# Cross-attention on one core: query row sums moved to TensorE, check products moved to batch 14, and the later queries split and spread by themselves

## What is computed

```python
Q = relu(queries @ Wq + bq);  K = relu(keys @ Wk + bk);  V = relu(values @ Wv + bv)
scores = einsum('hbqd,hbkd->hbqk', Qh, Kh) * scale
key_mask = sign(abs(sum(keys, axis=-1)))
scores = where(key_mask == 0.0, NEG, scores)
attn = softmax(scores, axis=-1)
q_mask = sign(abs(sum(queries, axis=-1)))
attn = attn * q_mask[..., None]
out = einsum('hbqk,hbkd->hbqd', attn, Vh)   # heads side by side again
return out + queries                         # queries is x; keys and values are both ctx_1024
```

## Time and profile before

| | |
|---|---|
| median of 3 runs | 380.84 us (379.0 to 381.56) |
| profiled execution, its own time | 380.48 us |
| its span, first to last instruction | 378.7 us |
| TensorE matmul busy | 357.3 us, 94% of the span |
| ScalarE busy | 303.9 us, 80% |
| VectorE busy | 240.4 us, 63% |
| GpSimd busy | 5.7 us, 2% |
| mean granted TensorE clock | 0.995 |

### The profile page before, as it was taken

One profiled execution on the slowest core, in us unless ns is written; L12 is line 12 of the kernel. 1 busy time (PEld: TensorE's weight loads), 2 busy tenths in 40 slices (PEclk: granted clock), 3 DMA queues, 4 the chain that ended last, 5 costly groups with the idle time before them and its releaser, 6 DMA issues.

```text
span 378.7 us, 16915 instructions
## 1 busy us (share of the span) xinstructions
PE 357.3 (94%) x6712; PEld 252.0 (67%) x6712; DVE 240.4 (63%) x785; ACT 303.9 (80%) x405; POOL 5.7 (2%) x20
## 2 busy tenths in 40 slices
PE   7997898799999999999999999999999999799991
PEld 5655666467676767676776767676776767577660
DVE  5797948267593939576684939485775937475202
ACT  2487477678888888888888888888888888689990
POOL 4010000000000000000000000000000000000000
PEclk9999999999999999999999999999999999999997
DMA  7529904956383745646373846547363837245100
GB/s 222 137 76 326 340 7 88 335 190 209 109 286 86 271 130 185 212 153 191 134 243 85 303 99 221 178 159 227 126 210 103 295 89 263 62 151 175 13 3 8
DMA packets 42852, 63.42 MB, mean 167 GB/s; under 512 B 28426, under 2 KB 32842, under 8 KB 42826
## 3 DMA queue, kind: packets, MB, share of 16 engines
q1 hardware_dynamic: 42106, 62.15, 51.8%
q10 hardware_dynamic: 720, 0.89, 0.7%
HBM read 14.55 MB, written 0.82 MB: 41 GB/s over the span
## 4 chain that ended last, share of the span: by engine, by line
PE 82%; DVE 6%; SPq 3%; DMA 3%; issue 2%; ACT 1%; DVEq 0%; ACTq 0%
PE psum L564 31%; PE psum L549 26%; PE psum L516 12%; PE psum L508 11%; SPq L334 3%; DMA k_parts<-k_low 3%; PE psum L636 1%; DVE v_biased L810 1%; PE psum L647 1%; DVE values L820 1%; DVE selectors L989 1%; ACT probs L477 1%; ACT k_parts L467 1%; DVE q_sum L946 1%; SPq L301 1%
## 5 line engine op out<-in xcount | busy, mean ns | idle before, releaser
L477 ACT ACTIVATE probs<-psum 128x800 f32<-128x800 f32 x384 | 293.5, 840 | 53.3 <-PE psum L549 53.3
L564 PE MATMUL psum<-probs,values 128*32 128x200 f32 x3072 | 153.7, 333 | 0.0
L549 PEld LDWEIGHTS psum<-query_bd,k_parts 64*128 64x128 f32 x1536 | 96.1, 187 | 44.9 <-issue 40.0
L564 PEld LDWEIGHTS psum<-probs,values 128*32 128x32 f32 x3072 | 97.8, 110 | 40.8 <-issue 19.1
L549 PE MATMUL psum<-query_bd,k_parts 64*128 64x200 f32 x1536 | 120.0, 286 | 1.6 <-DMA k_parts<-k_low 1.4
L773 DVE TENSOR_SCALAR_CACHE_REDUCE k_raw<-psum,bk_sb 128x361 f32<-128x361 f32 (+2 forms) x63 | 37.7, 600 | 88.3 <-PE psum L508 88.2
L508 PE MATMUL psum<-keyT,wk_mixed 128*32 128x361 f32 (+2 forms) x504 | 52.4, 491 | 6.2 <-DMA keyT<-in_ctxT 2.2
L516 PE MATMUL psum<-wv_sb,keyT 128*32 128x129 f32 x1536 | 55.1, 277 | 3.3 <-DVE v_biased L810 3.3
L820 DVE TENSOR_SCALAR values<-v_biased,keep 128x128 f32<-128x128 f32 x192 | 43.8, 289 | 6.4
L516 PEld LDWEIGHTS psum<-wv_sb,keyT 128*32 128x32 f32 x1536 | 38.4, 109 | 10.8 <-DVE v_biased L810 4.0
L810 DVE TENSOR_TENSOR v_biased<-psum,bv_sb 128x384 f32<-128x384 f32 x64 | 35.1, 548 | 0.0
(11 more groups left out here) (64 smaller groups left out, 81.7 us busy)
## 6 DMA issues: line engine op xcount, KB each, us to landing
k_parts<-k_high SPq DMA_DIRECT2D x30, 722.0 KB, 5.0
k_parts<-k_low SPq DMA_DIRECT2D x30, 722.0 KB, 5.5
keyT<-in_ctxT SPq DMA_DIRECT2D x15, 722.0 KB, 4.4
query_rep<-k_parts SPq DMA_DIRECT2D x4, 800.0 KB, 8.0
residual<-in_x SPq DMA_DIRECT2D x64, 12.5 KB
out<-residual SPq DMA_DIRECT2D x64, 12.5 KB
x_sb<-in_x SPq DMA_DIRECT2D x1, 800.0 KB
values<-in_xT ACTq DMA_DIRECT2D x1, 600.0 KB, 6.7
```

The source lines that it names most:

```text
L477: nc.scalar.activation(probs[:, u % PROB_SLOTS], scores_ps[:, u % SCORE_SLOTS, :, 0:QCOLS], ACT.Exp, scale=SCALE).then_inc(probs_ready, 1)
L549: mm = nc.tensor.matmul(scores_ps[:, u % SCORE_SLOTS, j, n * TCOLS:(n + 1) * TCOLS], k_parts[rows, parity, t, kt * P:(kt + 1) * P], query_ ...
L564: mm = nc.tensor.matmul(o_spans[c * VCOLS:(c + 1) * VCOLS, half, :, :, 0:SPAN], values[:, parity, kt, half * HALF_PAIRS + c, :], probs[:, ...
```

## The change

The line numbers of the diff's minus side are those of the kernel before. What it does:

- **Row sums by TensorE.** x is no longer loaded to `x_sb`, and the two sums on VectorE go. In cycle 0 of batch 0, behind the first scores and ahead of the first key quarter, TensorE multiplies the 16 blocks of `xT_sb` (128 x 100) with a column of ones into `work_ps` (`sum_queries`). VectorE compares them with zero. In cycle 7 of batch 0 TensorE multiplies the mask with a 0/1 matrix `row_pick`, which GpSimd makes, in 4 matmuls (`pick_rows`), and VectorE copies the result to `row_mask`. The 16 small DMAs go.
- **Check products in batch 14.** `k_max` gets a column for each batch. `q_max`, all 16 products and the head sums are made once, behind the last values of batch 14.
- **Later queries apart.** `q_high` and `q_low` hold only batches 0 to 3, and the four DMAs at L351 copy those alone. Batches 4 to 15 get `late_high` and `late_low`, made by VectorE between the key quarters of batch 2 in batch 0, and four more DMAs, which SyncE issues behind `spread_keys(2, 0)`. `batch(b, ...)` on VectorE waits for them ahead of `spread_queries(b + 1, ...)`, in every batch from 1 on.
- **Order at the start.** Weights are mixed ahead of the selectors on VectorE. On ScalarE's DMA queue bk comes first, then the first block of xT, then Wq, bq and the rest of xT. On SyncE the loads of `residual` for batches 0 and 1 come right behind the first evacuations.
- **First batch on VectorE.** Reading and masking values is woven between the steps of the key split.

```diff
-            def spread_masks():
-                sp.wait_ge(q_masked, 1)
-                sp.wait_ge(pads_zeroed, 4)
-                ... 16 DMAs row_mask<-q_mask
@@ SyncE
             load_keys(1, 1)
-            sp.dma_start(x_sb[:], x.rearrange("b q d -> q b d")).then_inc(x_loaded, 16)
-            sp.wait_ge(q_relued, 2)
-            for ready, count, source, slots in ((q_high_ready, 1, q_high, (0, 1)), (q_split, 3, q_low, (2, 3))):
+            sp.wait_ge(pads_zeroed, 4)
+            sp.wait_ge(first_evacuated, KCHUNKS)
+            load_residual(0, 0)
+            load_residual(1, 1)
+            for ready, count, source, slots in ((q_relued, 2, q_high, (0, 1)), (q_split, 2, q_low, (2, 3))):
...
             spread_keys(1, 1)
-            spread_masks()
-            load_residual(0, 0)
-            load_residual(1, 1)
-            sp.wait_ge(work_filled, KPARTS + VGROUPS)
+            sp.wait_ge(work_filled, SUMS + KPARTS + VGROUPS)
             load_keys(3, 1)
             sp.wait_ge(scores_ready, UNITS)
             spread_keys(2, 0)
+            for ready, source, slots in ((late_high_ready, late_high, (0, 1)), (late_split, late_low, (2, 3))):
+                sp.wait_ge(ready, 1)
+                for n in slots:
+                    sp.dma_start(query_rep[n:P:SLOTS, :, QB * SQ:].bitcast(F32),
+                                 source[:].rearrange("p g n -> p (g n)").bitcast(F32)).then_inc(late_replicated, 16)
@@ GpSimd
+            nc.gpsimd.memset(row_pick, 1.0).then_inc(rows_picked, 1)
+            nc.gpsimd.affine_select(out=row_pick, in_=row_pick, ...).then_inc(rows_picked, 1)
@@ TensorE
+            def sum_queries(index):
+                work(index)
+                for b in range(B):
+                    mm = nc.tensor.matmul(work_ps[0:SQ, b:b + 1], xT_sb[:, b * SQ:(b + 1) * SQ], ones[:, 0:1],
+                                          start=True, stop=True)
+                mm.then_inc(work_filled, 1)
+            def pick_rows(index):
+                work(index)
+                pe.wait_ge(rows_picked, 2)
+                for g in range(SPANS):
+                    mm = nc.tensor.matmul(work_ps[:, g * B:(g + 1) * B], row_pick[:, g, :], q_mask[:],
+                                          start=True, stop=True)
+                mm.then_inc(work_filled, 1)
...
-            FIRST_SIDE_WORK = (((0, NEXT),), ((1, NEXT), (2, NEXT)), ((3, NEXT), VALUES[0]), VALUES[1:2], VALUES[2:3],
-                               (VALUES[3], KEYS[0]), KEYS[1:3], KEYS[3:4])
+            FIRST_SIDE_WORK = (((SUM, NEXT), (0, NEXT)), ((1, NEXT), (2, NEXT)), ((3, NEXT), VALUES[0]), VALUES[1:2],
+                               VALUES[2:3], (VALUES[3], KEYS[0]), KEYS[1:3], (KEYS[3], (ROWS, NEXT)))
@@ VectorE
-            def bound_scores(b, parity):
-                at = slice(b, b + 1) if isinstance(b, int) else bass.ds(b, 1)
-                v.tensor_tensor(bound_terms[:, at], k_max[:, parity:parity + 1], q_max[:, at], ALU.mult
-                                ).then_inc(bound_made, 1)
+            def bound_scores():
+                v.tensor_reduce(q_max[:], queryT[:].rearrange("p (b q) -> p b q", b=B), AX.X, ALU.max
+                                ).then_inc(q_maxed, 1)
+                dve.wait_ge(q_maxed, 1)
+                dve.wait_ge(k_max_ready, 2 * B)
+                v.tensor_tensor(bound_terms[:], k_max[:], q_max[:], ALU.mult).then_inc(bound_made, 1)
...
@@ VectorE, batch(b, ...) from batch 1 on
+                dve.wait_ge(late_replicated, 16 * SLOTS)
                 spread_queries(b + 1, 1 - parity)
                 finish_keep(b + 1, 1 - parity)
-                bound_scores(b + 1, 1 - parity)
```

More of the change, by code:

```diff
@@ L127, in attention @@
         k_chunk_max = sb("k_chunk_max", [P, KPARTS])
-        k_max = sb("k_max", [P, 2])
+        k_max = sb("k_max", [P, B])
+        late_high = sb("late_high", [P, QGROUPS - 1, QB * SQ], F32R)
+        late_low = sb("late_low", [P, QGROUPS - 1, QB * SQ], F32R)
         v_biased = sb("v_biased", [P, VGROUPS, VGROUP, D])
@@ L387, in general @@
             def general(b):
+                sp.dma_start(g_x, row(x, b)).then_inc(g_x_loaded, 16)
                 sp.dma_start(keyT[:, 0, 0:SK], row(ctxT, b)).then_inc(g_loaded, 16)
@@ L594, in side_work @@
                     k, ahead = step
-                    if keys or ahead == NEXT:
+                    if k == SUM:
+                        sum_queries(used)
+                        used = used + 1
+                    elif k == ROWS:
+                        pick_rows(used)
+                        used = used + 1
+                    elif keys or ahead == NEXT:
                         prepare(b + ahead, (parity + ahead) % 2, k, used)
@@ L600, in batch @@
                     units = range(cycle * CYCLE, (cycle + 1) * CYCLE)
-                    for step in side[cycle][:-1]:
+                    early = 0 if first and cycle == 0 else max(len(side[cycle]) - 1, 0)
+                    for step in side[cycle][:early]:
                         side_work(step)
@@ L607, in batch @@
                         pe.wait_ge(first_k_spread, KCHUNKS * QUADS)
-                    for step in side[cycle][-1:]:
+                    for step in side[cycle][early:]:
                         side_work(step)
@@ L868, in finish_outputs, with split_keys @@
                 v.tensor_tensor(residual[:, parity], residual[:, parity], o_norm[:], ALU.add).then_inc(out_ready, 1)
[L870 to L880 removed]
+            def split_keys(b, used):
+                max_keys(b, used)
+                turn_outputs(b - 2)
+                dve.wait_ge(k_replicated, 16 * SLOTS * (b - 1))
+                center_keys(k_high, b, k_high_ready)
+                center_keys(k_cent, b, k_cent_ready)
             def finish_keys(b, part):
@@ L909, in first_batch @@
                 spread_queries(1, 1)
+                finish_values(1, 1, 3, used + 3)
                 finish_keep(1, 1)
-                bound_scores(0, 0)
-                bound_scores(1, 1)
-                sum_heads()
                 used = used + VGROUPS
-                for c in range(KPARTS):
-                    read_keys(2, c, used + c)
-                split_keys(2, 0, used + KPARTS)
-                dve.wait_ge(rows_masked, 16 * HALF_PAIRS * SPANS)
+                read_keys(2, 0, used)
+                high_queries()
+                read_keys(2, 1, used + 1)
+                read_keys(2, 2, used + 2)
+                low_late_queries()
+                read_keys(2, 3, used + 3)
+                used = used + KPARTS
+                read_rows(used)
+                split_keys(2, used)
             def batch(b, parity, last=False, keys=True):
@@ L937, in batch @@
                         read_keys(b + 2, c, used + c)
-                    split_keys(b + 2, parity, used + KPARTS)
+                    split_keys(b + 2, used + KPARTS)
                 else:
+                    bound_scores()
+                    sum_heads()
                     turn_outputs(b)
-            def sum_queries(part):
-                rows = slice(part * B // 2, (part + 1) * B // 2)
-                dve.wait_ge(x_loaded, 16)
-                v.tensor_reduce(q_sum[:, rows], x_sb[:, rows], AX.X, ALU.add).then_inc(q_summed, 1)
@@ new lines, in low_first_queries, with low_late_queries @@
+            def low_first_queries(at):
+                v.tensor_tensor(q_low[:, at], queryT[:, at], q_high[:, at].bitcast(F32), ALU.subtract
+                                ).then_inc(q_split, 1)
+            def high_queries():
+                dve.wait_ge(q_relued, 1 + QGROUPS)
+                v.tensor_copy(late_high[:].rearrange("p g n -> p (g n)"), queryT[:, QB * SQ:]
+                              ).then_inc(late_high_ready, 1)
+            def low_late_queries():
+                dve.wait_ge(late_high_ready, 1)
+                v.tensor_tensor(late_low[:].rearrange("p g n -> p (g n)"), queryT[:, QB * SQ:],
+                                late_high[:].rearrange("p g n -> p (g n)").bitcast(F32), ALU.subtract
+                                ).then_inc(late_split, 1)
```

143 lines of the change are left out of this document (62 added, 81 removed).

## The result

The changed kernel takes 391.24 us in the median of 4 runs (389.49 to 393.58), beside 380.63 us for the kernel before (379.0 to 381.56): a ratio of 1.0305, 95% interval 1.0259 to 1.0351. It is slower, and it lies outside the range of the prediction. The profiled execution took 393.58 us with a span of 391.8, 13.1 more than the span before, at a mean granted clock of 0.963 (before 0.995). It is the slowest of the four runs, 2.3 us above their median.

The account below looks back on a forecast made before the run. TensorE was taken as the bound, at 21.07 us a loop batch, with only the start and batches 0 and 1 affected. A net +2.9 us at batch 2's start, added to 380.5, gave 383.4 us, range 379.6 to 387.5.

Parts of the forecast that it names:

- Start: Before batch 0: mixing goes ahead of the casts but Wq lands later, TensorE beginning at about 6.8 us; +0.4 us.
- Sums of queries: Batch 0, ahead of the first key quarter: 32 weight loads on TensorE, hidden by nothing; 2.7 us, from 1.8 to 3.5.
- my +0.3: Batch 0's net change after sums, picking, new waits and freed old waits; +0.3 us, from -0.7 to +1.2.
- Rows picked: Last cycle of batch 0: 4 TensorE matmuls, 8 passes of 128 loaded columns; 0.9 us.
- Batch 1, what goes: VectorE's mask wait, batch 3's late keys and SyncE's delay of batch 2's keys vanish; batch 1 alone would take 21.1 us.
- Batch 1, what comes: VectorE waits for late copies landing at 73.2, TensorE waits 7.0 us; net +2.9 us at the start of batch 2.
- rival 2: Batch 1: late copies crawl at 258 GB/s, landing at 76.3; 386.5 us, 388 with upper bounds elsewhere; chance 0.20.
- Batches 2 to 14 at nothing: Loop batches' small extra VectorE work fits about 0.6 us of slack, batch 14's checks fit 7.08 us idle; no cost.
- rival 3: Near the end, VectorE's batch 13 stall moves to where it has time; 381.3 us, 2.1 less; chance 0.10.
- my three signs of being wrong: SyncE issues late copies before the low keys are ready, they exceed 400 GB/s, or a loop batch changes.

Follow-up runs that it names:

- experiment 1: Changed kernel with SyncE issuing the four late query copies ahead of the key pair of batch 2; 379.14 us, 0.9967 of the kernel before.
- experiment 4: Changed kernel with each of the 16 sum matmuls moving 32 columns of ones in place of one; 390.5 us, 1.0269 of the kernel before.
- experiment 5: Changed kernel with 42 unread filler matmuls on TensorE ahead of batch 1's second key quarter, its batches 1 and 2 written out; 388.16 us, 1.0233 of before.
- experiment 6: Kernel before with only its 16 mask copies replaced by TensorE's row picking; 377.32 us, 0.9911 of the kernel before.
- Experiment 2: Changed kernel without VectorE's wait for the late copies in batches 1 and 2, those batches written out on VectorE; 378.4 us, 0.9954 of before.
- the wide sums: Sum matmuls moving 32 columns of ones in place of one: on the changed kernel 390.5 us, with late copies ahead of the key pair 378.98 us.
- experiment 7: Changed kernel with late copies ahead of the key pair, x loaded again and its row sums made by one VectorE reduction; 375.84 us, 0.9873 of before.
- experiment 3: Changed kernel with one matmul of 16 columns in place of the 16 sum matmuls, for timing alone; 386.13 us, 1.0154 of the kernel before.
- experiment 9: As experiment 7, but x asked for later, behind the last key chunk of batch 0; 374.41 us, 0.9874 of the kernel before.
- experiment 8: As experiment 7, but the start's loads and weight mixing in the order of the kernel before; 376.12 us, 0.9891 of the kernel before.
- the repetition of experiment 1: Changed kernel with late copies ahead of the key pair and one-column sums, run again beside the wide sums on the same chip; 379.06 us.
- experiment 10: As experiment 9, but VectorE's loop over batches 1 to 12 written out; 370.79 us, 0.9774 of the kernel before.

## Why the prediction was wrong

The mechanism named in it was right at every link of batch 1; its sizes were not, and one whole term was missing. In spans, my sum held +0.4 + 0.3 + 2.2 (batch 1) = +2.9, and the profile shows +13.1.

- *Start*: taken at +0.4, measured +0.6, and TensorE began at 6.71 (I had 6.8). Part of this is luck. Wq landed at 5.92, not at 6.55, and then its copy took 0.71 us beside GpSimd's pattern selection, where the copy before took 0.26. And two things move the first full product from profile to profile by more than the term: whether the first projection takes 0.94 or 1.70 us, and the half clock from 8 to 11. Like beside like, the new order costs what I took: 25.61 against 25.06 where the projection takes 1.70 (experiment 1, before), 24.17 and 24.24 against 23.73 where it takes 0.94 at full clock (experiments 4 and 5 against 6). Experiment 2, where the later xT kept TensorE waiting, is left out of this.
- *Sums of queries*: 2.7 us taken, 4.15 measured; with the clock at 1.00 they take 3.0 (0.094 a load, from the wide sums). The loads were sized nearly right; at a falling clock the same ones took 1.15 more and the matmuls behind them 1.8 more (31.97 - 28.99 = 2.98 in all; in three of the five profiles only 1.4 to 1.6). With the full clock batch 0 would be +0.7, against my +0.3. Rows picked: 0.9 taken, 1.07 measured.
- *Batch 1, what goes*: right. No wait for keyT, for k_parts or for the mask copies; experiment 6 shows it alone.
- *Batch 1, what comes*: the low keys were ready 6.7 us behind the transposing, as I had it (57.85 to 64.58). From there to the last landing I took 12.2 us and it took 14.3, that is 2.1 more. The likeliest place of these is visible, not tested: I gave the queue 5.6 us for the key pair and then only bytes, but SyncE alone needed from 64.61 to 71.16 to ask for the copies, and the last took 7.67 from there. As a rate, 3.94 MB in 14.3 us is 276 GB/s, nearer to rival 2's 258 than to the 322 of my 12.2 us.
- *The term that was missing*: TensorE's clock. Behind the wait it cost 2.4 (experiment 5), during and behind the sums 3.0 in this profile (experiment 4).
- *Batches 2 to 14 at nothing*: a loop batch stayed at 21.07 and batch 14 hid its new work. Rest grew by 2.1 in this profile: batch 13 took 25.20 us and not 23.26, as its stall was 0.3 longer and the clock fell behind it where it had not before. That is rival 3's place with the other sign, and chance has a part in it: experiments 1, 2 and 5 have the stall without the half clock.

Together, from prediction to profile: 0.2 + 3.4 + 2.1 + 2.4 + 2.1 = 10.2, and 383.4 + 10.2 = 393.6, the profiled execution. The failed step is that I gave the matmuls behind the wait and behind the sums the lengths of their rows of before, so that TensorE's clock stood in the sum at nothing. The half clock makes 3.0 + 2.4 + 1.6 = 7.0 of the 10.2 us in this profile, the late landing 2.1. In the median of the four runs the time is 7.8 above the forecast, and the scatter of these clock terms is the likeliest reason that it is less than 10.2 (argued, not shown). Rival 2, slower copies, was nearly right about the landing and had the right sign; its sizes without the clock ended at 388. None of my three signs of being wrong appeared (early copies, over 400 GB/s, another loop batch), so they would not have caught the error.

Beyond the sizes, I took the wait on `late_replicated` in batches 1 and 2 as given by the data. It isn't. Had I asked which queries are the first to lie in the late columns (those of batch 4, which VectorE spreads in batch 3), the fix would have stood in the prediction.

The price of the parts, as far as the runs separate them: the picked rows give some 3 us (experiment 6). The rest of VectorE's new order in batch 0, that is the later split of the queries, the woven values, the moved check products and one sum in place of two, gives a further 3.6 us (29.25 - 25.63, experiments 6 and 7); these four were not separated. The TensorE sums take back 5.1 us by the medians of experiment 3, 6.3 by batch 0 of the profile (31.97 - 25.63) and 3.3 by the medians of experiments 1 and 7. The early wait costs 12 (experiment 1).

## What to carry over

When work is taken out of a transfer queue and other work put in, write down for each wait which iteration first reads what it guards: here a wait two iterations early cost 12 us, although the copies themselves cost nothing. When a change leaves TensorE idle for several us, or gives it matmuls that no row of before resembles, read the granted clock behind them, and keep a second term for it (here 2.4 us behind 9.1 us of waiting, and 1.4 to 3.0 with the sums). Compare batch lengths, not totals, since the second cost can fall elsewhere, and compare medians of two chips only through the kernel before on each. When TensorE is the bound, a small reduction is cheaper on an engine that is idle at that place, as VectorE was in experiment 7.

## What the runs showed of the hardware

- Granted clock: with 9.12 us of idleness TensorE was granted 1.00 up to 75 us and 0.50 from 76 to 86; with fillers 1.00 throughout. With one moving column a weight load of 100 columns stepped 0.093 us at 1.00 (2.99 us for 32, experiment 1), and the clock fell to 0.50 in five of five profiles; with 32 columns the step was 0.094 and it fell in none of two.
- Shorter idle times have no certain price. TensorE idled 1.7 to 2.8 us at the stall near the end in the thirteen profiles that have one. Behind it the granted clock fell to 0.50 in seven (the changed kernel, experiments 6 to 9 and both with wide sums) and stayed at 1.00 in six. At the start it fell behind 1.83 and 1.87 us of idleness (the changed kernel and the repetition of experiment 1), where the first key projection then took 4.33 and 4.30 us; with 0.8 to 1.7 us of idleness it stayed at 1.00 in all others.
- At a granted clock of 1.00 the first projection (two passes of 400 columns) took 1.70 us in some profiles (before, experiment 1) and 0.94 in others (experiment 6, at 6.49 us). Experiments 1 and 4 have the same program up to the first full product, which came at 25.61 us (projection 1.70) and at 24.17 (projection 0.94). So 1.4 us between two profiles at the start need not be the effect of an edit.
- In every kernel with a VectorE loop, VectorE stood once behind it with nothing to wait for: 3.1 to 3.8 us in batch 13, and in experiment 2, whose loop begins two batches later and ends at the same one, 1.94 us at the start of TensorE's batch 14. With its loop written out it did not stand at all (experiment 10).
- In experiment 8 a VectorE copy of 128 columns began at 6.22 us, while GpSimd's pattern selection ran from 6.03 to 6.89, and took 0.77 us; the next one, behind the selection, took 0.25. In the kernel before, where GpSimd was idle, both took 0.25 to 0.26. The Trainium skill, SBUF — State Buffer, section "Who interferes with whom", says that a copy in VectorE's two-port mode and a GpSimd operation lock each other out for a whole instruction. This trace agrees.
